# Taking the units of the expert layer in pairs on TensorE

## What is computed

```python
x = x + _L0_conv_ref(_ln_c(x), L0_conv_w)
t = _to_tokens(x)                      # 32 x 256 tokens of D = 64
logits = xf @ gate_w + gate_b          # xf = _ln_t(t); E = 8 experts
probs = softmax(logits); top2_vals, top2_idx = top_k(probs, 2)
cw = zeros.at[..., top2_idx].add(top2_vals)
for each expert e:                     # H = 128
    h = gelu(xf @ W1[e] + b1[e]); y = h @ W2[e] + b2[e]
    acc = acc + cw[:, e, None] * y
x = x + acc
```

## Time and profile before

| | |
|---|---|
| runs, median of 3 | 219.78 us (218.99 to 220.37) |
| the profiled execution, its own time | 218.63 us |
| its span, first to last instruction | 216.7 us |
| granted TensorE clock, mean | 0.95 |
| TensorE busy | 188.4 us, 87% |
| DVE, ACT, POOL busy | 63%, 48%, 53% |
| DMA | 22.36 MB |

### The profile page before, as it was taken

The page is one execution under the profiler, slowest core; times in us unless marked ns, Lnnn a source line. Parts: engine busy times, 40 slices in busy tenths (PEclk is TensorE's granted clock), DMA queues, the critical chain, the costliest instruction groups (busy, mean ns, idle before and its releaser), DMA issues.

```text
span 216.7 us, 3237 instructions
## 1 busy us (share of the span) xinstructions
PE 188.4 (87%) x859; PEld 73.1 (34%) x859; DVE 137.1 (63%) x436; ACT 104.8 (48%) x140; POOL 115.5 (53%) x108
## 2 busy tenths in 40 slices
PE   2966105999979989999999999999999999999990
PEld 2954101566766335422222222222222222222220
DVE  0999999996759655754754664663773763334342
ACT  2539700333372724396465555645555465554640
POOL 7696007799000024456565665756656565665663
PEclk9999755999995899999999999999999999999998
DMA  6940000000000593970890890693692593495101
GB/s 175 316 71 3 0 2 0 0 3 0 3 0 1 142 201 79 202 166 7 209 224 11 203 213 28 152 204 88 166 206 67 143 207 91 124 200 120 50 0 48
DMA packets 16176, 22.36 MB, mean 103 GB/s; under 512 B 2202, under 2 KB 7970, under 8 KB 16162
## 3 DMA queue, kind: packets, MB, share of 16 engines
q1 hardware_dynamic: 16002, 22.04, 45.0%
q10 hardware_dynamic: 160, 0.15, 0.2%
HBM read 19.82 MB, written 2.36 MB: 102 GB/s over the span
## 4 chain that ended last, share of the span: by engine, by line
PE 74%; DVE 14%; issue 4%; DMA 2%; ACT 2%; POOL 1%; POOLq 1%; DVEq 1%; ACTq 0%
PE ps L956 30%; PE ps L971 27%; PE ps L889 8%; PE ps L846 3%; PE ps L929 3%; DVE ssum L566 2%; DVE xn L578 2%; DMA cw<-in_conv_w 2%; PE ps L916 2%; DVE topi L715 1%; DVE gbc L613 1%; PE ps L944 1%; DVE xn L617 1%; DVE cw_x L601 1%; DVE cw_max L539 1%
## 5 line engine op out<-in xcount | busy, mean ns | idle before, releaser
L370 POOL TENSOR_TENSOR x<-x,y_sb 128x512 f32 (+1 forms) x63 | 80.2, 1272 | 79.2 <-DVE y_sb L754 79.1
L494 ACT ACTIVATE work<-ps,bias_sb 128x1024 f32<-128x1024 f32 x64 | 71.2, 1114 | 62.9 <-PE ps L956 62.9
L754 DVE SCALAR_TENSOR_TENSOR y_sb<-ps,bias_sb,gbc 128x512 f32<-128x512 f32 x64 | 48.0, 750 | 59.4 <-PE ps L971 56.5
L956 PE MATMUL ps<-xT,w_sb 64*128 64x512 f32 x256 | 73.4, 650 | 0.1
L971 PE MATMUL ps<-work,w_sb 128*64 128x512 f32 x256 | 68.8, 617 | 0.1
L956 PEld LDWEIGHTS ps<-xT,w_sb 64*128 64x128 f32 x256 | 19.6, 188 | 43.4 <-issue 42.4
L971 PEld LDWEIGHTS ps<-work,w_sb 128*64 128x64 f32 x256 | 12.8, 134 | 48.5 <-issue 37.7
L889 PE MATMUL ps<-qpad,cw_bd 128*128 128x512 bf16 x72 | 18.6, 410 | 10.2 <-POOL qpad L340 10.2
L340 POOL TENSOR_TENSOR qpad<-work,xn 128x512 bf16<-128x512 f32 (+1 forms) x8 | 11.1, 1401 | 7.4 <-issue 7.4
L389 ACT ACTIVATE work<-ps 128x512 f32<-128x512 f32 x16 | 9.3, 596 | 10.9 <-PE ps L846 10.9
L889 PEld LDWEIGHTS ps<-qpad,cw_bd 128*128 128x128 bf16 x72 | 7.2, 101 | 19.4 <-issue 12.6
(11 more groups left out here) (88 smaller groups left out, 140.3 us busy)
## 6 DMA issues: line engine op xcount, KB each, us to landing
gbc<-gate_rows SPq DMA_DIRECT2D x16, 768.0 KB, 9.7
gbc<-gate_rows SPq DMA_DIRECT2D x16, 256.0 KB, 4.1
x_sb<-in_x SPq DMA_DIRECT2D x8, 256.0 KB, 5.5
out<-x SPq DMA_DIRECT2D x8, 256.0 KB, 9.7
w_sb<-in_W SPq DMA_DIRECT2D x3, 256.0 KB, 6.9
gate_rows<-gateT SPq DMA_DIRECT2D x8, 32.0 KB, 1.9
cw<-in_conv_w ACTq DMA_DIRECT2D x2, 72.0 KB, 3.7
gate_bd<-in_gate_w SPq DMA_DIRECT2D x2, 2.0 KB, 6.1
```

Of the source, the lines that this page charges most:

```text
L370: pool.tensor_tensor(x2[:, ds(c * W, W)], x2[:, ds(c * W, W)], y_sb[:, u % H_RING, :], ALU.add).then_inc(added, 1)
L494: act.activation(h_sb[:, u % H_RING, :], bank(H + 2 * (u % 2), 2 * W), ACT.Gelu, bias=b1_sb[:, u:u + 1]).then_inc(gelu_done, 1)
L754: dve.scalar_tensor_tensor(y_sb[:, u % H_RING, :], bank(Y + u % 2), b2_sb[:, u:u + 1], gbc[:, slot, u, :], ALU.add, ALU.mult).then_inc(wei ...
L956: last = pe.matmul(bank(H + 2 * (u % 2) + r), w1_sb[r * CH:(r + 1) * CH, u * HIDDEN:(u + 1) * HIDDEN], xT[r * CH:(r + 1) * CH, ds(c * W, W ...
```

## The change

TensorE's order in the expert layer is written for two units at a time: first products of u and u + 1, then second products of u - 2 and u - 1. Inside a product, nothing is changed, nor is any buffer or any other engine's order. The gates of the next chunk are transposed behind the first pair of second products, where they were transposed after the same second product before. In chunk 0 the transpositions of `x2` and the logits follow in twos and in fours.

```diff
             def ffn(c, gates=True, first=False):
-                for u in range(UNITS):
+                for u in range(0, UNITS, 2):
                     first_product(c, u)
+                    first_product(c, u + 1)
                     if u >= G2_LAG:
                         second_product(c, u - G2_LAG)
+                        second_product(c, u + 1 - G2_LAG)
                     elif not first:
                         second_product(c - 1, u - G2_LAG + UNITS)
-                    if u == 1 and gates and not first:
+                        second_product(c - 1, u + 1 - G2_LAG + UNITS)
+                    if u == 0 and gates and not first:
                         transpose_gates(c + 1)
                     if first:
 
@@
                             transpose_gates(1)
                         if u < NCH - EARLY:
                             transpose_x2(EARLY + u)
-                        elif u < NCH - EARLY + 2:
+                            transpose_x2(EARLY + u + 1)
+                        elif u == NCH - EARLY:
 
                             pe.wait_ge(gateT_ready, 2)
-                            logits(2 * u - EARLY)
-                            logits(2 * u - EARLY + 1)
+                            for k in range(EARLY, NCH):
+                                logits(k)
```

## The result

| | us, median | ratio to before, 95% interval |
|---|---|---|
| before, 4 runs | 219.38 (218.01 to 220.37) | |
| changed, first set | 211.58 (208.84 to 279.01, 4 runs) | 0.9555 [0.9476, 0.9635] |
| changed, second set | 209.23 (208.88 to 210.37, 4 runs) | 0.9555 [0.9515, 0.9594] |
| changed, third set | 209.29 (207.81 to 213.85, 6 runs) | 0.9544 [0.9480, 0.9608] |

The kernel became 4.5% faster; 209.9 us was forecast. In the executions of 213.72 us (the profiled one of the first set), 279.01 us (mean clock 0.643, no trace of it is kept) and 213.85 us the chip granted TensorE less clock, and the ratios are taken without them. The profile read here is that of the second set (208.88 us, span 207.1).

A forecast was written before the change was run, and what follows sets the result against it. TensorE was taken to bound the kernel; steady part -9.5, start -0.9 and end +0.5 sum to -9.9 us, from the median 219.78 to 209.9 us (73%). Own range 208.2 to 211.7, whole range 208.0 to 216.0.

The forecast's parts named there:

- A change of product costs a gap and a bare load: TensorE between first and second products: 0.10 us gap, plus an unhidden weight load of 0.10 (first) or 0.05 us (second).
- parts "what a change costs" and 1: The prediction's sections on the cost between unlike products on TensorE, and on the steady part, 9.5 us less.
- Two first products hide each other's loads: Inside a pair of first products on TensorE: weights load behind the running round, 0.20 us less per pair, bounds 0 and 0.20.
- Rival 1: First products of a pair don't hide each other's loads, only second products gain: 216.1 us; chance 8%.
- Steady part -9.5: Unit 2 of chunk 1 to unit 7 of chunk 7: 27 pairs, each 0.35 us less, 9.5 us.
- Others keep up, 0.3 us spare on DVE: ACT, DVE, POOL and DMA feed the pairs without stall; tightest is DVE's weighing ahead of second product 7.
- rival 2: One more router operation held up behind a POOL add stalls TensorE once per chunk, 4.4 us in all: 214.3 us; chance 9%.
- Start -0.9: 68.8 to 96.8 us: transposition waits +1.8, filled idle ahead of the gates -1.1, fewer product changes -1.6; bounds +1 and -2.
- -1.6 by the forecast: Within the start: four pairs at 0.35 us, and two product changes fewer around the transpositions at 0.1 us.
- four logits in a row at no cost: In the start: the logits of four chunks in a row cost what they did before.
- End +0.5: Kernel's end: POOL's adds pile up behind paired second products, 5.4 us instead of 4.82, so 0.5 us more.
- The forecast's own range: 208.2 to 211.7 us, from the start's bounds and 0.01 us reading error in each of four rounds (1.1 us).

The follow-up runs named there:

- the inserted matmuls: Four kernels: the changed kernel plus one unread 16-column matmul inside each of 24 pairs; same layout 0.9602 and 0.9548 of before, differing layout 0.9843 and 0.9773.
- the longer router: The changed kernel plus two unread 128x512 reductions on DVE behind the router's steps after unit 4; one run 214.48 us (0.9755), the other three 219.5 us.

## Why the prediction was right

- *A change of product costs a gap and a bare load (parts "what a change costs" and 1).* Right, and shown by the inserted matmuls: gap 0.10 to 0.11 us (0.10 was read), loads 0.10 and 0.05 (0.10 and 0.05). The four rounds at the kernel's end had carried all of it.
- *Two first products hide each other's loads, for which there was no row.* Right: 0.43 in each middle round. Rival 1 has fallen, and with it, for both layouts, the rule that the prediction cites from the Trainium skill (TensorE: Matmul & The Clock Gate, Part 3, "The mechanism"): loads on the same rows as the running matmuls were hidden.
- *Steady part -9.5.* From unit 2 of chunk 1 to the second product of unit 5 in chunk 7 it was 208.66 - 96.76 = 111.90 us and is (197.57 + 0.91) - 96.09 = 102.39: -9.5.
- *Others keep up, 0.3 us spare on DVE.* Right: TensorE has no wait in the steady part, and the longer router gave 1.2 - 0.93 = 0.3 us. One operation did fall behind an add as in rival 2, L704 in chunk 0 (0.70 instead of 0.18 us), where nobody waited for it.
- *Start -0.9.* 27.94 us from the first product to unit 2 of chunk 1 before, 27.04 after: -0.9. The terms were there: the second transposition waits 0.9 us twice (73.39 to 74.25 in the chain above), and the wait of 1.10 us ahead of the gates is gone. In the rest, -1.6 by the forecast and by these rows, there is luck. The forecast counted four pairs of first products where five lie in this part (units 0 to 7 of chunk 0, 0 and 1 of chunk 1), which is worth 0.2 us more. Against that, the half clock at the start reached 3.7 us into the expert layer in this execution and 3.4 before, which cost 0.2. The forecast also put four logits in a row at no cost; that holds in six of ten profiles, and in the other four a half-clock stretch of 3.3 us goes with them.
- *End +0.5.* 6.25 us from the second product of unit 4, where 6.3 was worked out: +0.5.
- *Sum.* -9.9 forecast. The span went from 216.7 to 207.1, 9.6 less, and 0.2 of the rest is that the expert layer began later (69.05 against 68.82). The forecast's own range, 208.2 to 211.7, can't be had again from the two terms that it names: added up they give 207.7 to 212.9. The measured medians lie in both.

## What to carry to other kernels

Where two kinds of matmul alternate that cut the array differently, read the distance between starts at a change and inside a run of one kind; the difference, here 0.2 us for 64x128 fp32 weights and 0.15 for 128x64, is what grouping gives back for each product that comes to lie behind one of its own kind, as long as the buffers let the other engines follow. Before grouping, lay the other engines' steps on the new times: here one engine had 0.3 us to spare, and it was found from a single row. And look at which small matmuls the new order collects in a row, here in the first chunk: half clock may meet them there, though these runs don't show that it is the row of them that brings it.

## What the runs showed of the hardware

- The gap between two layouts of the array is 0.10 to 0.11 us at the full clock of 2.4 GHz, between row halves and all rows as well as between column halves and row halves, and with a matmul of 16 columns as with rounds of 512.
- Weight loads of the same layout are hidden by a running 512-column round, for row halves and for full-height column halves. The Trainium skill (TensorEngine Tiling (Array Packing), "Key Properties") says that changing the tiling mode, not just the tile, drains TensorE; the runs agree in that each change costs time, and give the 0.10 to 0.11 us.
- Waits on semaphores that are already satisfied cost TensorE nothing that these runs can tell, even three and more ahead of each product (1.92 and 1.87 us for two products, as without them).
- Half clock, the 1.2 GHz level, came for 6.8 us behind the logits in the first profile (88.7 to 95.5). Before the clock fell TensorE had run matmuls of 16 columns for 2.5 us (86.11 to 88.7), and had idled 0.9 us ahead of the last transposition (81.70). Other executions of the same kernel kept the full clock through the same steps.
- A DVE operation of 128x64 with two inputs (L737) took 1.25 us where an add of POOL began beside it and 0.23 us where POOL was idle; it ended within 0.1 us of the add.
